# A graph layer on one core: the first six spans are counted behind four visits, TensorE reads its table in the gate blocks, and there are five pair places

## The reference

```python
agg = segment_sum(x[src], dst, num_segments=6250)
h = relu(agg @ W_rel + b_rel + x @ W_root)            # 256 -> 512
i, f, g, o = split(h @ W_ih.T + b_ih + b_hh, 4)        # f is not used
c = sigmoid(i) * tanh(g)
out = layernorm(x + (sigmoid(o) * tanh(c)) @ W_fc + b_fc)
```

## Time and profile before

| | us |
|---|---|
| median of 3 runs | 1827.25 (1826.65 to 1827.99) |
| the profiled execution's own time | 1824.41 |
| its span, first to last instruction | 1822.5 |
| TensorE busy | 1513.5 (83%) |
| GpSimd busy | 1281.0 (70%) |
| VectorE busy | 815.9 (45%) |
| ScalarE busy | 418.5 (23%) |
| mean granted TensorE clock | 0.910 |

### The profile page before, as it was taken

One profiled execution on the slowest core, in us unless ns is written; L12 is line 12 of the kernel. 1 busy time (PEld: TensorE's weight loads), 2 busy tenths in 40 slices (PEclk: granted clock), 3 DMA queues, 4 the chain that ended last, 5 costly groups with the idle time before them and its releaser, 6 DMA issues.

```text
span 1822.5 us, 31499 instructions
## 1 busy us (share of the span) xinstructions
PE 1513.5 (83%) x6882; PEld 1213.0 (67%) x6883; DVE 815.9 (45%) x1763; ACT 418.5 (23%) x743; POOL 1281.0 (70%) x1926
## 2 busy tenths in 40 slices
PE   0157688697988898788998889899988888999997
PEld 0023355486767676667887667688876676888886
DVE  8877666431322654531324565422244654222332
ACT  0001021110112332220222333212223332222333
POOL 5875877777777877877777668776763668656640
PEclk9976677698988998889999999999998998999999
DMA  9563555576766555567766445576652455766540
GB/s 342 209 233 87 150 161 145 157 225 207 215 195 180 162 162 165 161 198 223 223 206 180 138 133 166 160 246 217 203 155 77 133 146 161 225 189 177 150 122 18
DMA packets 131966, 319.14 MB, mean 175 GB/s; under 512 B 17295, under 2 KB 68268, under 8 KB 130198
## 3 DMA queue, kind: packets, MB, share of 16 engines
q0 software_dynamic: 75264, 245.95, 46.4%
q10 hardware_dynamic: 52632, 54.80, 9.5%
q1 hardware_dynamic: 3936, 16.62, 2.4%
HBM read 298.10 MB, written 19.20 MB: 174 GB/s over the span
## 4 chain that ended last, share of the span: by engine, by line
PE 48%; POOL 21%; issue 19%; DVE 4%; DMA 3%; DVEq 3%; POOLq 1%; ACT 0%; ACTq 0%; SPq 0%
PE ps_blk L537 20%; POOL rows L400 14%; PE ps_agg L476 9%; PE ps_win L464 6%; POOL idx L370 6%; PE ps_y L545 4%; PE ps_blk L519 3%; PE ps_blk L524 3%; PE ps_tr L451 1%; DMA hot_key<-in_xb 1%; POOL rows L385 1%; PE ps_win L451 1%; DMA rows<-x_parts,idx 1%; POOLq L370 1%; DMA wih_sb<-in_x 1%
## 5 line engine op out<-in xcount | busy, mean ns | idle before, releaser
L400 POOL DMA_INDIRECT rows<-x_parts,idx x924 | 963.5, 1043 | 453.5 <-PE ps_agg L476 157.6
L537 PE MATMUL ps_blk<-cell,wih_sb 128*128 128x250 f32 x2400 | 545.5, 385 | 2.9 <-issue 2.2
L537 PEld LDWEIGHTS ps_blk<-cell,wih_sb 128*128 128x128 f32 x2400 | 464.1, 196 | 69.5 <-issue 8.8
L476 PE MATMUL ps_agg<-rows,onehot 128*125 x1112 | 341.8, 462 | 153.2 <-SPq L339 70.8
L476 PEld LDWEIGHTS ps_agg<-rows,onehot 128*125 128x125 f32 x1112 | 234.1, 216 | 227.5 <-issue 175.9
L906 DVE SCALAR_TENSOR_TENSOR onehot<-iota_f,tile_first,dst_u 128x500 f32 (+1 forms) x278 | 207.0, 746 | 291.7 <-PE ps_agg L476 171.6
L370 POOL COPY idx<-src_sb 128x1 int32 x956 | 264.4, 277 | 16.7 <-issue 9.7
L664 ACT ACTIVATE cell<-ps_blk,bg_sb 128x250 f32<-128x250 f32 x300 | 140.8, 470 | 544.0 <-PE ps_blk L537 470.2
L897 DVE TENSOR_TENSOR hot_key<-iota_h,rel 128x980 f16 x263 | 174.4, 663 | 0.4 <-issue 0.4
L464 PE MATMUL ps_win<-adj,hot_key 128*128 128x250 f32 x784 | 170.7, 375 | 2.4 <-DMA hot_key<-in_xb 1.5
L464 PEld LDWEIGHTS ps_win<-adj,hot_key 128*128 128x128 f32 x784 | 148.0, 190 | 21.6 <-DMA hot_key<-in_xb 4.0
(11 more groups left out here) (125 smaller groups left out, 914.2 us busy)
## 6 DMA issues: line engine op xcount, KB each, us to landing
hot_key<-in_xb ACTq DMA_DIRECT2D x28, 896.0 KB
rows<-x_parts,idx POOLq DMA_INDIRECT x924
x_t<-in_xT ACTq DMA_DIRECT2D x25, 250.0 KB
x_n<-in_x ACTq DMA_DIRECT2D x25, 250.0 KB
out<-y ACTq DMA_DIRECT2D x25, 250.0 KB
x_parts<-wih_sb SPq DMA_DIRECT2D x4, 1024.0 KB, 6.8
wih_sb<-in_x ACTq DMA_DIRECT2D x6, 512.0 KB, 9.7
x_parts<-cell SPq DMA_DIRECT2D x2, 1024.0 KB, 7.6
```

What stands on the lines that cost most here:

```text
L400: g.indirect_dma_start(rows_f[:, k * QC + j, :], None, x_parts, bass.IndirectOffsetOnAxis(ap=idx[:, k, j:j + 1], axis=0)).then_inc(landed[ ...
L476: ins = mm(o, onehot[:, hot * QC + j, 0:TN], rows[:, ds(slot + j, 1), :].squeeze(1), start=(first and j == 0), stop=False)
L537: last = mm(o, wih_sb[:, k, col:col + P], h_t[:, k, :], start=(k == 0), stop=(k == KH - 1))
```

## The change

- **Head.** VectorE makes four one-hots (`FIRST_HOTS = 4`) with the splits of raw steps 0 to 3, then the pairs of the first six spans, with the splits of steps 4, 5 and 6 behind the first, the second and the third span. TensorE does visits 0 to 3, then the three windows, then visits 4 and 5 and so on. The splits share one scratch area in `cell` instead of two in `adj`.
- **Table loads of TensorE.** The counts of pairs of both spans of a window are packed into one word (`T_WINDOW`); `load_windows()` loads one word for each window and takes it apart with two register operations, in the second gate block of the part, together with the load of the next part's number of steps. The pair loop runs from 0 to the count.
- **Table loads of VectorE.** `load_span()` for the next span stands in the body of the pair loop, between `hot_lo` and `hot_key`, and so runs once for each pair. `unpack()` keeps its three register operations.
- **Pair places.** `PAIRS` goes from 4 to 5. `next_place()` has five register operations in place of the four of `next_pair()`; the step of the pair counter is apart (after the loop on TensorE, in it on VectorE).
- **Source indices.** `src_sb` (int32) becomes `src_u` (uint16), cast by VectorE at the start; GpSimd waits for that cast and copies its index columns from it. The int32 data lie in the ring's last slot until VectorE has read them.

```diff
-PAIRS = 4
+PAIRS = 5
...
-FIRST_HOTS = 3
+FIRST_HOTS = 4
...
-        src_sb = sb("src_sb", [P, CHUNK_COLS], i32)
+        src_u = sb("src_u", [P, CHUNK_COLS], u16)
...
-        def unpack(engine, regs, at):
+        def load_span(engine, regs, at):
+            engine.reg_load(regs[0], table[0:1, at:at + 1] if isinstance(at, int) else table[0:1, ds(at, 1)])
+
+        def unpack(engine, regs):
             packed, first, past = regs
-            engine.reg_load(packed, table[0:1, at:at + 1] if isinstance(at, int) else table[0:1, ds(at, 1)])
...
-        def next_pair(engine, pair, place, more):
-            engine.reg_add(pair, pair, 1)
+        def next_place(engine, place, past_last):
+            engine.reg_add(past_last, place, 2 - PAIRS)
+            engine.reg_alu(past_last, past_last, 0, ALU.max)
+            engine.reg_alu(past_last, past_last, -PAIRS, ALU.mult)
             engine.reg_add(place, place, 1)
-            engine.reg_alu(more, place, PAIRS, ALU.is_lt)
-            engine.reg_alu(place, place, more, ALU.mult)
+            engine.reg_add(place, place, past_last)
...
-            pool.wait_ge(edges_in, 32)
+            pool.wait_ge(src_short, 1)
...
-                g.tensor_copy(idx[:, k % RING, j:j + 1], src_sb[:, ds(chunk + j, 1)]).then_inc(idx_copied, 1)
+                g.tensor_copy(idx[:, k % RING, j:j + 1], src_u[:, ds(chunk + j, 1)]).then_inc(idx_copied, 1)
...
+                if k == RING - 1:
+                    pool.wait_ge(src_read, 2)
...
+            def load_windows(w0, n_windows):
+                for i in range(n_windows):
+                    at = w0 + (T_WINDOW + i)
+                    even, odd = window_pairs[i]
+                    pe.reg_load(counts_of, table[0:1, at:at + 1] if isinstance(at, int) else table[0:1, ds(at, 1)])
+                    pe.reg_alu(even, counts_of, PACK, ALU.python_divide)
+                    pe.reg_alu(odd, counts_of, PACK, ALU.python_mod)
+
             def windows(w0, n_windows):
                 for i in range(n_windows):
-                    w = w0 + i
                     bank = (ps_win, ps_tr)[i % 2]
-                    pe.wait_ge(win_evac, w + (2 if i == 0 else 1))
+                    pe.wait_ge(win_evac, w0 + (i + (2 if i == 0 else 1)))
                     mm(bank[:, 0:SCOLS], zero_bf[:, 0:P], zero_bf[:, 0:SCOLS], start=True, stop=False)
                     for side in range(2):
                         o = bank[:, side * SCOLS:(side + 1) * SCOLS]
-                        first, past = unpack(pe, pe_regs, at)
-                        with pe.Fori(first, past, QC):
-                            s = pe.snap(pair_0, min_val=0, max_val=MAX_PAIRS)
+                        n = pe.snap(window_pairs[i][side], min_val=1, max_val=STEPS)
+                        s0 = pe.snap(pair_0, min_val=0, max_val=MAX_PAIRS)
+                        with pe.Fori(0, n) as m:
+                            s = pe.snap(m + s0, min_val=0, max_val=MAX_PAIRS)
...
-                            next_pair(pe, pair_0, place, more_places)
+                            next_place(pe, place, past_last)
+                        pe.reg_add(pair_0, pair_0, n)
...
-            def part_sum(t, a, part):
+            def load_part(t, a, part):
+                at = t + ((T_MORE_A, T_MORE_B)[part] + a)
+                pe.reg_load(more_steps, table[0:1, at:at + 1] if isinstance(at, int) else table[0:1, ds(at, 1)])
+
+            def part_sum(t, a, part, between=None):
                 o = ps_agg[a][0:TN, :]
-                col = (T_MORE_A, T_MORE_B)[part] + a
-                more = pe.value_load(table[0:1, t + col:t + col + 1] if isinstance(t, int) else table[0:1, ds(t + col, 1)], min_val=1, max_val=STEPS - 1)
+                more = pe.snap(more_steps, min_val=1, max_val=STEPS - 1)
...
-                with pe.Fori(0, more, HOTS) as i:
+                done = 0
+                if between is not None:
+                    done = FIRST_HOTS - 1
+                    for i in range(1, FIRST_HOTS):
+                        visit(o, pe.snap(s0 + i, min_val=1, max_val=MAX_STEPS), pe.snap(u0 + i, min_val=0, max_val=MAX_VISITS), i)
+                    between()
+                with pe.Fori(done, more, HOTS) as i:
...
-                                  (p + 1 - part) % HOTS)
+                                  (p + 1 - part + done) % HOTS)
...
-            def gates(n, j):
+            def gates(n, j, load_next=None):
...
+                    if which == 1 and load_next is not None:
+                        load_next()
...
+                def first_windows():
+                    load_windows(w, wins[0])
+                    windows(w, wins[0])
+
                 for j in range(KH):
+                    def load_next():
+                        load_windows(w, wins[j])
+                        if j + 1 < KH and parts[j + 1] is not None:
+                            load_part(t, *parts[j + 1])
+
                     if parts[j] is not None:
-                        part_sum(t, *parts[j])
-                    if not first:
-                        gates(n - 1, j)
+                        if j == 0 or (j == 1 and parts[0] is None):
+                            load_part(t, *parts[j])
+                        part_sum(t, *parts[j], between=first_windows if first and j == 0 else None)
+                    if first and j == 0:
+                        load_part(t, *parts[1])
+                    elif first:
+                        load_next()
+                    else:
+                        gates(n - 1, j, load_next)
                     if wins[j] > 0:
-                        windows(w, wins[j])
+                        if not (first and j == 0):
+                            windows(w, wins[j])
...
-                at, raw_top = ds(k * QC, QC), raw_tops[k % 2]
+                at = ds(k * QC, QC)
                 for j in range(QC):
                     dve.wait_ge(landed[k][j], 16)
-                if k >= 2:
-                    dve.wait_ge(gathered, RING + k - 1)
+                if k >= 1:
+                    dve.wait_ge(gathered, RING + k)
...
+            dve.wait_ge(edges_in, 32)
+            v.tensor_copy(src_u[:, :], src_i).then_inc(src_short, 1)
...
+            sides = hi.rearrange("p (w s) -> p w s", s=2)
+            v.scalar_tensor_tensor(table[:, T_WINDOW:T_WINDOW + WINDOWS], sides[:, :, 0], float(PACK), sides[:, :, 1], ALU.mult, ALU.add).then_inc(setup, 1)
+            n_setup[0] += 1
+            dve.wait_ge(setup, n_setup[0])
...
-            dve.wait_ge(edges_in, 32)
             v.tensor_copy(dst_u[:, :], dst_i).then_inc(setup, 1)
-            v.tensor_scalar(src_part, src_sb[:, :], P - 1, None, ALU.bitwise_and).then_inc(setup, 1)
-            v.tensor_scalar(src_high, src_sb[:, :], P.bit_length() - 1, None, ALU.logical_shift_right).then_inc(setup, 1)
-            n_setup[0] += 3
+            v.tensor_scalar(src_part, src_i, P - 1, None, ALU.bitwise_and).then_inc(src_read, 1)
+            v.tensor_scalar(src_high, src_i, P.bit_length() - 1, None, ALU.logical_shift_right).then_inc(src_read, 1)
+            n_setup[0] += 1
             dve.wait_ge(setup, n_setup[0])
+            dve.wait_ge(src_read, 2)
...
             place = dve.alloc_register("place")
             dve.reg_mov(place, 0)
+            load_span(dve, dve_regs, T_SPAN)
...
-                first, past = unpack(dve, dve_regs, at + T_SPAN)
+                first, past = unpack(dve, dve_regs)
...
+                    load_span(dve, dve_regs, at + (T_SPAN + 1))
...
-                    next_pair(dve, pair_0, place, more_places)
+                    dve.reg_add(pair_0, pair_0, 1)
+                    next_place(dve, place, past_last)
...
-                more = dve.value_load(table[0:1, t + col:t + col + 1] if isinstance(t, int) else table[0:1, ds(t + col, 1)], min_val=1, max_val=STEPS - 1)
+                dve.reg_load(more_steps, table[0:1, t + col:t + col + 1] if isinstance(t, int) else table[0:1, ds(t + col, 1)])
+                more = dve.snap(more_steps, min_val=1, max_val=STEPS - 1)
...
-                    windows_at(w, wins, j)
+                    if made == 0 or j > 0:
+                        windows_at(w, wins, j)
...
-            for k in range(RING):
+            for k in range(FIRST_HOTS):
                 split_gathered(k)
-                if k < FIRST_HOTS:
-                    visit(0, dve.snap(0 * group0 + k), dve.snap(0 * group0 + k), k * QC)
+                visit(0, dve.snap(0 * group0 + k), dve.snap(0 * group0 + k), k * QC)
+            for i in range(2 * FIRST_SLOTS[0]):
+                span(i // 2, i % 2)
+                if FIRST_HOTS + i < RING:
+                    split_gathered(FIRST_HOTS + i)
+
```

21 lines of the change are left out of this document (14 added, 7 removed).

## The result

The changed kernel takes 1767.16 us (median of 4 runs, 1764.15 to 1770.68) against 1826.95 in the same comparison for the kernel before (1825.66 to 1827.99): ratio 0.9674, 95% interval 0.9653 to 0.9694, some 60 us faster. I had said 1810 and 1792 to 1828. The sign was right, the size was not, by more than the range.

What follows compares the result with a forecast made beforehand. GpSimd's gathers were taken to bound 152 to 862, TensorE's own stream from there; head +10, stall -3, windows -20 and clock -4 gave -17, so 1827.25 became 1810 us, range 1799 to 1821 (0.60), outer 1792 to 1828.

Steps and rivals of the forecast that it cites:

- the loads only move: Rival: TensorE pays for divide, remainder and longer pair loop what it saves in loads, head stays late; 1834, chance 0.10.
- The windows' 20 us: TensorE's window stages: 50 windows of groups 2 and 3 save 0.4 us each, 20 us, bounds 12 and 30.
- The clock: TensorE's two late window stages: shorter gaps spare some drops of the granted clock, 4 us, bounds 0 and 12.
- Groups 0 and 1, nothing: Windows of groups 0 and 1 lie in GpSimd's stretch and save nothing.
- The head, 10 us,: Head: slower VectorE pairs and a slot not free make gather step 12 10 us later, bounds 1 and 18.
- The 3 us: GpSimd's stall of 2.98 in front of 657.62, waiting for TensorE, gives back up to 3 us; bounds 0 and 3.
- The fifth place: Fifth pair place lets VectorE finish a part's pairs sooner; its gain lies in the windows' bounds.
- The 16-bit copies: GpSimd's index copies from uint16, taken at no cost; rival: slower, 1831 at 0.05 us a copy, chance 0.07.
- The cap by VectorE: Rival: VectorE becomes the bound in the late windows, capping the windows' gain near 12 us; 1818, chance 0.06.

Runs made afterwards that it cites:

- e14: The kernel before with TensorE's unpacked span words loaded behind the first gate product, not in front of each span's loop; nothing packed: 1785.41 us, ratio 0.9776.
- e1: e0 with TensorE's window words and part counts loaded directly in front of their windows and parts, not in the gates: 1815.45 us, ratio 0.9932.
- e7: e0 with each window's word loaded twice in the gate block, once for each side: 1816.47 us, ratio 0.9946.
- e8: e0 with the first window word loaded behind the first gate product, the others and the next part's count behind the second: 1772.84 us, ratio 0.9713.
- e12: The changed kernel with a one-instruction clamp behind each of its table loads, in place of e0's bounds assertions: 1762.30 us, ratio 0.9661.
- e15: The kernel before with one edit, 16-bit source indices cast once by VectorE and copied by GpSimd: 1822.87 us, ratio 0.9989.
- e0: The changed kernel with a bounds assertion behind each table load of TensorE and VectorE, base of other kernels: 1773.76 us, ratio 0.9706.
- e4: e0 with VectorE loading each span's packed word in front of the span's loop, not inside the pair body: 1771.92 us, ratio 0.9702.
- e2: e0 with the head in the order of the kernel before: 1774.51 us, ratio 0.9700.
- e5: e4 with the head in the order of the kernel before as well, e2's edit: 1775.48 us, ratio 0.9727.
- e3: e0 with four pair places instead of five: 1771.52 us, ratio 0.9683.
- e9: e0 with only the head's six spans loading their word in front of the loop, later spans inside the body: 1765.28 us, ratio 0.9676.

## Why the prediction was wrong

**The step that failed** is this sentence: "Moving a load in front of the gates' last blocks is no gain in itself, since one sequencer does all of it in turn and begins each part without a lead; only what it no longer does counts." I had the lead in the gates in front of me (I wrote 3.4 us; 1075.39 less 1071.8 is 3.6) and didn't ask whether it could have been longer. It could not: the sequencer stood still for 1.2 us of the gate block. Work put there is free up to that. e14 moves loads and does nothing else, and takes 40 us less than the kernel before; e1 takes the move away from the changed kernel (42 us), and e7 and e8 show its limit. The rival "the loads only move", to which I gave 0.10 and 1834, had the right edit and the wrong sign.

**How the 60 us come together.** The two stretches in which groups 2 and 3 have their windows, each from its first gate product to that of the turn behind it, hold the same matmuls in every kernel. In the kernel before, in the changed one and in e14 (columns as in the earlier trace rows):

```profile
995.57:1189.80 194.23, 169.28 (x820) 133.52 (x819) 105.00 (x248) 62.51 (x102) 142.69 (x208) 0.95 0.53 151
1360.11:1555.61 195.50, 170.21 (x809) 134.99 (x807) 104.64 (x246) 62.72 (x102) 122.91 (x177) 0.91 0.46 131
```

```profile
987.87:1165.44 177.57, 163.43 (x820) 131.28 (x819) 110.16 (x250) 61.20 (x102) 130.43 (x197) 0.95 0.55 158
1333.43:1499.33 165.90, 157.54 (x808) 127.05 (x807) 108.62 (x248) 62.05 (x102) 109.97 (x164) 0.98 0.50 142
```

```profile
990.30:1170.36 180.06, 160.42 (x821) 129.29 (x819) 107.06 (x252) 62.73 (x102) 138.82 (x200) 0.97 0.55 157
1336.76:1516.14 179.38, 159.48 (x808) 128.51 (x807) 106.20 (x250) 62.70 (x102) 117.89 (x169) 0.96 0.48 135
```

The changed kernel needs 46 us less for the two, and e14 30 less. What the lowered clock can have cost is at most (1 - clock) x length, an estimate: 27 us before, 12 after, 13 in e14. So up to 15 of the 46 us are the clock's, and at least 31 are left for the shorter gaps; of e14's 30 us, at most half are the clock's. Taken from one part's first gate product to the next part's, and only where both kernels ran at full clock, a two-window part wins 1.4 to 2.3 us in the changed kernel (six parts) and 0.9 to 1.5 in e14 (five parts), and the latter fits the standstill. With three windows, and so six words, e14 wins nothing and loses up to 1.8.

**The windows' 20 us** were 31 at the least, at the upper bound of 30. The price of a load was low: I took 0.05 + 0.30 and the unpacking, busy times, where the starts in the earlier trace rows stood there to be read. In e7 a further word costs 0.8. What the packing adds on top of the move is at most e14 less e12, 23 us, with all the rest of the change in it; where the loads stand in the open (e1) it adds nothing to a two-window part.

**The clock.** I had 4 us, bounds 0 and 12, and it can have given up to 15. It goes with the gaps: e1, e7 and e15, whose parts are as long as those before, lose up to 22, 22 and 36 us to it by the same estimate, and the kernels with shorter parts 3 to 12. That longer gaps and a lower clock go together is shown; why they do is not. My price for it was misread as well. Twelve matmuls of visits took 5.06 us at half clock in the earlier trace rows, but at full clock they take 3.1 (e1's line at 1076.56) and not half.

**Groups 0 and 1, nothing.** I had the kernel 7 us late in front of group 2's windows, and it was 5.2 early. By the visits it goes from 1.0 late to 8.9 early while group 1's windows are counted (595 to 809 in the kernel before). e14, with GpSimd's program and the head unchanged, goes from 1.5 late to 3.7 early there. So the move pays in GpSimd's stretch too. These 12 us, the 11 or more of the windows and up to 11 of the clock make up most of the 43 us that the forecast lacks.

**The head, 10 us,** was 6.2 at step 12, well inside its bounds, and my account of it (pairs of 1.5, slots that aren't free) held. I took it for the price of the new order together with the longer body, and it is the body's: under the new order the load in it costs 7.2 us (e0 less e4), under the old one 0.9 (e2 less e5), and the order wins 5.8 without that load (e5 less e4) and nothing with it (e2 less e0). That the lateness would last up to 862 and the end did not hold: step 60 begins at 479.02, when it did before (479.07), and e2 ends with e0. What takes it up was not tried.

**The 3 us** at 657.62 came, and 3 more of the same kind; e7, whose windows are slow again, has 10.1 us of such waits. GpSimd's stretch isn't free of TensorE's windows.

**The fifth place** brings nothing (e3). **The 16-bit copies** aren't slower; whether they are faster stays open. The cap by VectorE didn't come.

## What to carry to other kernels

A sequencer that runs ahead of its array has idle time exactly where the array's work is long, and the busy rows don't show it: look for a stretch without register instructions between the last of a dense block and the first of what follows, and put loads there, up to the array work that is queued in front of them. Moving them further along gains nothing (e8), and putting in more than fits costs again (e7). Price a register load by the distance from one start to the next, not by its duration. A load in a loop's body is paid for each time round where that engine sets the pace; take it out there. Whether it is better left in elsewhere is not settled here (e9 and e4 differ by 0.26%, with intervals that overlap). And look at TensorE's granted clock beside its gaps: here the kernels with the longer gaps also had the lower clock, and the same matmuls took longer.

## What the runs showed of the hardware

- TensorE's sequencer passes eight matmul pairs in 0.3 us when it may (1057.0 to 1057.3), and stood still for 1.2 us with the array 3.7 us behind it. In 14 of 17 parts it went on with 3.95 us of gate work, 18 pairs of 128x250 in f32, still ahead of the array. Whether that number holds for other shapes wasn't tried.
- The Trainium skill, Advanced Engine Details and Errata, section Sequencer Loop, says that engine instructions are pushed into a queue, that a control instruction starts executing in ucode, and that other engine instructions can be read and queued meanwhile. The first agrees with the lead of 3.95 us. The last isn't what e7 shows for matmuls behind register loads: the array ran out of them and stood for 2.01 us.
- At half clock (granted 0.50) twelve matmuls of visits took 5.48 us (the kernel before, at 1510.00), at full clock 3.12 (e1, at 1076.56).
- A wait in the profile can name an engine that isn't its cause: e14's 1.01 behind the first gate product stands under ScalarE.
